# Written orders for the first two and last three head groups, a second set of probability tiles for the last group, and a shorter last row in a transposing attention kernel

## What is computed

```python
xn = layernorm(x)                                # x: 4 x 512 x 256, float32
Q = xn @ Wq + bq; K = xn @ Wk + bk; V = xn @ Wv + bv   # 16 heads of 128; 4 for K and V
attn = softmax(Q K^T / sqrt(128) + causal mask)
y = gelu((attn V) @ Wo + bo)
s = layernorm(xn + y) * gamma + beta
g = silu(ffn(xn))                                # gate/up 2 x 1024, down to 256
out = x + s * g
```

## Time and profile before

| | |
|---|---|
| median of the runs | 644.49 us (643.44, 648.06, 644.49) |
| profiled execution | 651.28 us, its span 649.5 us |
| mean granted TensorE clock | 0.978 |
| PE busy, PEld busy | 609.5 us (94%), 525.8 us (81%) |
| DVE, ACT, POOL busy | 479.2 us (74%), 428.7 us (66%), 304.1 us (47%) |

### The profile page before, as it was taken

How to read it: one execution, slowest core, us unless ns; L and a number is a source line. 1 busy time by engine, 2 the same in 40 slices (tenths; PEclk the granted TensorE clock), 3 DMA queues, 4 the chain that set the end, 5 groups by cost and what they waited for, 6 DMA issues and landing times.

```text
span 649.5 us, 10475 instructions
## 1 busy us (share of the span) xinstructions
PE 609.5 (94%) x3342; PEld 525.8 (81%) x3342; DVE 479.2 (74%) x1087; ACT 428.7 (66%) x1023; POOL 304.1 (47%) x243
## 2 busy tenths in 40 slices
PE   6899999999799999999999999999999999999771
PEld 4688888888678889788988888897988989798650
DVE  5654556543888778778988787898878889887736
ACT  2434344534788688677978777797877879787440
POOL 0000000000055654555689645468964546897544
...
GB/s 240 129 130 33 66 97 62 3 73 10 143 236 212 200 227 245 227 221 164 176 191 251 252 224 219 214 170 188 228 267 232 195 247 155 204 227 269 216 100 32
DMA packets 72501, 113.28 MB, mean 174 GB/s; under 512 B 11136, under 2 KB 50176, under 8 KB 70400
## 3 DMA queue, kind: packets, MB, share of 16 engines
...
q10 hardware_dynamic: 688, 0.33, 0.2%
...
## 4 chain that ended last, share of the span: by engine, by line
PE 62%; DMA 19%; DVE 7%; POOL 4%; ACT 4%; SPq 2%; issue 2%; ACTq 0%; POOLq 0%
PE bank L982 22%; PE down_ps L982 11%; DMA p_scratch<-probs 10%; PE down_ps L1112 8%; DMA probs<-p_scratch 7%; PE down_ps L1022 7%; PE bank L1011 6%; PE bank L1009 6%; POOL pT_lo L555 3%; DVE probs L915 3%; DMA raw<-in_wgu 2%; SPq L478 2%; PE bank L1073 2%; ACT pT_hi L698 1%; ACT probs L688 1%
## 5 line engine op out<-in xcount | busy, mean ns | idle before, releaser
L555 POOL TENSOR_TENSOR pT_lo<-probs,pT_hi 128x512 fp32r<-128x512 f32 x160 | 204.5, 1299 | 91.9 <-ACT pT_hi L698 91.4
L688 ACT ACTIVATE probs<-probs,least 128x512 f32<-128x512 f32 (+3 forms) x256 | 141.2, 554 | 37.6 <-DVE least L900 37.2
L900 DVE CUSTOM_DVE_ANT_0 probs<-bank,mask 128x512 f32<-128x512 f32 (+3 forms) x256 | 115.8, 484 | 24.9 <-PE bank L982 23.1
L698 ACT ACTIVATE pT_hi<-probs 128x512 fp32r<-128x512 f32 x160 | 96.1, 626 | 27.4 <-DMA probs<-p_scratch 21.1
L567 POOL TENSOR_TENSOR probs<-probs,inv 128x1024 f32<-128x1024 f32 (+1 forms) x32 | 47.0, 1469 | 141.1 <-DVE inv L908 141.0
L915 DVE STREAM_TRANSPOSE probs<-probs 128x2048 f32<-128x2048 f32 (+1 forms) x64 | 95.6, 1493 | 0.3 <-POOL probs L567 0.3
L1112 PE MATMUL down_ps<-wo_lo,cT_hi 128*128 128x256 f32 x256 | 74.4, 291 | 6.4 <-DVE cT_lo L940 6.3
L1112 PE MATMUL down_ps<-wo_hi,cT_lo 128*128 128x256 f32 x256 | 72.6, 284 | 0.0
L1112 PE MATMUL down_ps<-wo_hi,cT_hi 128*128 128x256 f32 x256 | 72.5, 283 | 0.0
L982 PE MATMUL down_ps<-pT_lo,v_hi 128*128 128x512 f32 x160 | 66.8, 417 | 6.0 <-POOL pT_lo L555 5.9
L982 PE MATMUL bank<-kT_lo,qT_hi 128*128 128x384 f32 (+1 forms) x192 | 66.4, 346 | 4.9 <-DVE least L900 3.3
...
## 6 DMA issues: line engine op xcount, KB each, us to landing
...
```

The costliest lines, as they stand in the source:

```text
L555: nc.gpsimd.tensor_tensor(lo[:].rearrange("p (a n) -> p a n", a=BLOCKS), turned(t, j), f32(hi[:]).rearrange("p (a n) -> p a n", a=BLOCKS), ...
L688: nc.scalar.activation(p, p, ACT.Exp, bias=least[:, u, g:g + 1], scale=-1.0, accum_out=total[:, n * T + t, g:g + 1]).then_inc(exp_done, 1)
L698: nc.scalar.activation(hi[:].rearrange("p (a n) -> p a n", a=BLOCKS), turned(t, j), ACT.Copy).then_inc(probsT_hi, 1)
L900: nc.vector.tensor_tensor_reduce(out=head_of(t, g), in0=ps[:, 0:(t + 1) * P].rearrange("p (k i) -> p k i", i=BLOCK), in1=mask_of(t), scale ...
```

## The change

The pattern stays for the middle. For the first two groups and the last three each engine gets a list of its own (`..._HEAD`, `..._TAIL`), and `program` puts them before and after what the pattern gives without them. What stands ahead of the last down product is now all of Q3, Q0, K, Q1, Q2; what stands ahead of `silu_out` on ScalarE is in `SCALAR_AHEAD`. The steps of the last row's end are in the lists too: `ty`, `ts`, `to` on VectorE (take y, statistics, output), `tg` (gelu), `tr` (root), `tp` (factors) and `td` (store).

The last group's probabilities get tiles of their own, in the space of Wq, with `gamma_g` and `beta_g`. Its masks so wait for the last projection and no longer for the `pl` of group 14. For the end, GpSimd makes g gamma and g beta + x ahead (`tile_factors`, three operations for each tile), and VectorE ends every tile with two operations.

```diff
+TENSOR_AHEAD = """
+Q3 Q0 K Q1 Q2
+"""
...
+SCALAR_AHEAD = """
+qh3 qh0 kh qh1 qh2 e2.0 e3.2 e3.1 e3.3 e3.0 e1.0 e2.2
+"""
...
+TRANSFER_HEAD = """
+W3 IW3 R3 W2 IR3 W0 IW2 R2 W1 IR2 R0 R1 W3+ R3+ W2+ IW3+ R2+ W1+ IR3+ W0+ IW2+ R1+
...
+def program(head, text, tail):
+
+    head, tail = [*listed(head, 0, 0)], [*listed(tail, LAST, B - 1)]
+    return head + [s for s in order(text) if s not in head and s not in tail] + tail
...
+    late = ExitStack()
+    probs_last = [sb(f"probs_last{t}", [P, G * (t + 1) * P], F32, late) for t in range(T)]
+    gamma_g = sb("gamma_g", [P, T, D], F32, late)
+    beta_g = sb("beta_g", [P, T, D], F32, late)
+    late.close()
     wq_s = pair("wq", [P, DC, H * E])
...
+        def tile_factors(t):
+
+            i = TILE_READY["tp", t]
+            pool.wait_ge(proj_done, max(PROJECTED["Q", LAST, h] for h in range(G)))
+            pool.wait_ge(g_b_in, 16 * B)
+            pool.wait_ge(x_b_in, 16 * B)
+            nc.gpsimd.tensor_tensor(beta_g[:, t, :], g_b[:, t, :], beta_row, ALU.mult).then_inc(tile_chain_pool, 1)
+            nc.gpsimd.tensor_tensor(gamma_g[:, t, :], g_b[:, t, :], gamma_row, ALU.mult)
+            pool.wait_ge(tile_chain_pool, i)
+            nc.gpsimd.tensor_tensor(beta_g[:, t, :], beta_g[:, t, :], x_b[:, t, :], ALU.add).then_inc(tile_ready, 1)
...
-        first = first_of("kh", "qh")
-        steps(ACT_STEPS[:len(first)])
+        steps(ACT_STEPS[:len(ACT_AHEAD)])
         silu_out(B - 1)
-        steps(ACT_STEPS[len(first):])
-        tile_gelu_of(1)
-        tile_gelu_of(0)
+        steps(ACT_STEPS[len(ACT_AHEAD):])
...
         def tile_output(t):
...
             r = res[:, t, :]
...
-            nc.vector.scalar_tensor_tensor(r, r, mv3[:, t, 0:1], gamma_row, ALU.subtract, ALU.mult).then_inc(tile_scaled, 1)
-            dve.wait_ge(tile_scaled, done + 1)
-            nc.vector.scalar_tensor_tensor(r, r, rstd3[:, t:t + 1], beta_row, ALU.mult, ALU.add).then_inc(tile_scaled, 1)
-            dve.wait_ge(tile_scaled, done + 2)
-            nc.vector.tensor_tensor(r, r, g_b[:, t, :], ALU.mult).then_inc(tile_scaled, 1)
-            dve.wait_ge(tile_scaled, done + 3)
-            nc.vector.tensor_tensor(r, r, x_b[:, t, :], ALU.add).then_inc(tile_out_dve, 1)
+            dve.wait_ge(tile_ready, TILE_READY["tp", t])
+            dve.wait_ge(tile_root, TILE_ROOT["tr", t])
+            nc.vector.scalar_tensor_tensor(r, r, mv3[:, t, 0:1], gamma_g[:, t, :], ALU.subtract, ALU.mult).then_inc(tile_scaled, 1)
+            dve.wait_ge(tile_scaled, TILE_OUT["to", t])
+            nc.vector.scalar_tensor_tensor(r, r, rstd3[:, t:t + 1], beta_g[:, t, :], ALU.mult, ALU.add).then_inc(tile_out, 1)
...
-                    if n and t in BY_DRAM:
+                    if n == LAST:
+                        dve.wait_ge(proj_done, max(PROJECTED["Q", n, h] for h in range(G)))
+                    elif n and t in BY_DRAM:
                         dve.wait_ge(probsT_split, PT_SPLIT["pl", n - 1, t, t])
```

More of the change, by code:

```diff
@@ new lines @@
+"""
+SCALAR_HEAD = """
+e0.2 e2.3 e0.3 vh3 e0.0 e1.2 e2.1 e1.3 e0.1 vh0 e1.1 vh1 kh+ qh3+ ph3.1 ph3.0 qh1+ ph3.2 qh2+ vh2 ph3.3 qh0+
+ph2.0 ph2.1 ph2.2 e3.2+ ch3 e3.3+ e3.1+ e3.0+ ph1.0 ph1.1 ph0.0 ch2 e2.3+ e1.0+ e1.2+ e1.3+ e2.0+ e2.2+ e2.1+
+e1.1+ e0.1+ kh++ e0.3+ e0.2+ e0.0+ ch1 qh0++ ph3.0+ ph3.2+ qh2++ ph3.1+ qh1++ ph3.3+ ch0
+"""
+SCALAR_TAIL = """
+qh3-- ph2.0--- ph2.1--- e3.1-- ph2.2--- e3.2-- ch3--- e3.3-- ph1.0--- e3.0-- ph0.0--- ph1.1--- gelu- e0.2--
+e1.1-- e2.3-- e2.1-- e2.2-- ch2--- e2.0-- e0.3-- e1.3-- e1.2-- e1.0-- e0.0-- qh2- ch1--- e0.1-- ph3.0-- qh0- kh-
@@ new lines @@
+"""
+POOL_HEAD = """
+no0 no1 pl3.1 pl3.0 pl3.2 pl3.3 pl2.0 pl2.1 pl2.2 pl1.0 pl1.1 pl0.0 no1+ no0+ pl3.0+ pl3.2+ pl3.1+ pl3.3+
+"""
+POOL_TAIL = """
+pl2.0--- pl2.1--- pl2.2--- pl1.0--- pl0.0--- pl1.1--- res- no1-- root- pl3.0-- no0-- pl3.1-- pl3.2-- pl3.3--
+pl2.0-- pl2.1-- pl2.2-- out0- pl1.0-- pl1.1-- pl0.0-- out1- out2- out3- out4- out5- no1- out6- pl3.0- out7-
+pl3.1- no0- pl3.2- pl3.3- pl2.0- pl2.2- pl2.1- pl1.0- no1 pl1.1- pl0.0- tp0 pl3.1 pl3.0 no0 pl3.2 pl3.3 pl2.0
+pl2.1 pl2.2 pl1.0 pl1.1 tp3 pl0.0 tr3 tp1 tr2 tp2 tr1 tr0
@@ L113, in order, with listed @@
                 yield (kind, n + shift, *which)
-def first_of(*kinds):
-    return [(kinds["KQ".index(step[0])], *step[1:]) for step in FIRST]
+def listed(text, kv, row):
+    for kind, which, shift, _ in words(text):
+        if kind in AT_END:
+            yield (kind, *which)
+        else:
+            yield (kind, (row if kind in TILE_ROWS else kv) + shift, *which)
 def ranks(steps, *kinds):
@@ L129, in ring_of @@
     return {s: (i % RING_BANKS, uses[i - RING_BANKS] if i >= RING_BANKS else None) for i, s in enumerate(uses)}
-def ahead(steps, first):
-    return [*first, *(s for s in steps if s not in first)]
-PE_STEPS = ahead(order(TENSOR_ORDER), list(FIRST))
-ACT_STEPS = ahead(order(SCALAR_ORDER), first_of("kh", "qh"))
-DVE_STEPS = ahead(order(VECTOR_ORDER), first_of("kl", "ql"))
-POOL_STEPS = list(order(POOL_ORDER))
-SP_STEPS = list(order(TRANSFER_ORDER))
+def program(head, text, tail):
+    head, tail = [*listed(head, 0, 0)], [*listed(tail, LAST, B - 1)]
+    return head + [s for s in order(text) if s not in head and s not in tail] + tail
+PE_AHEAD, ACT_AHEAD = [*listed(TENSOR_AHEAD, 0, 0)], [*listed(SCALAR_AHEAD, 0, 0)]
+PE_STEPS = program(TENSOR_AHEAD + TENSOR_HEAD, TENSOR_ORDER, TENSOR_TAIL)
+ACT_STEPS = program(SCALAR_AHEAD + SCALAR_HEAD, SCALAR_ORDER, SCALAR_TAIL)
+DVE_STEPS = program(VECTOR_HEAD, VECTOR_ORDER, VECTOR_TAIL)
+POOL_STEPS = program(POOL_HEAD, POOL_ORDER, POOL_TAIL)
+SP_STEPS = program(TRANSFER_HEAD, TRANSFER_ORDER, TRANSFER_TAIL)
+TILE_Y = ranks(DVE_STEPS, "ty")
+TILE_GELU = ranks(ACT_STEPS, "tg")
+TILE_VAR = ranks(DVE_STEPS, "ts")
+TILE_ROOT = ranks(POOL_STEPS, "tr")
+TILE_READY = ranks(POOL_STEPS, "tp")
+TILE_OUT = ranks(DVE_STEPS, "to")
 RING = ring_of(PE_STEPS)
@@ L264, in build, with probs_of, by_blocks, head_of @@
     ctx_banks = [down_ps[:, 2, :], down_ps[:, 3, :]]
[L266 to L270 removed]
+    def probs_of(n, t):
+        return (probs_last if n == LAST else probs)[t]
+    def by_blocks(n, t):
+        return probs_of(n, t)[:].rearrange("p (k g i) -> p k g i", g=G, i=BLOCK)
+    def head_of(n, t, g):
         if t in BY_DRAM:
[L273 to L278 removed]
+            return by_blocks(n, t)[:, :, g]
+        return probs_of(n, t)[:].rearrange("p (g k i) -> p g k i", g=G, i=BLOCK)[:, g]
+    def turned(n, t, j):
+        return probs_of(n, t)[:].rearrange("p (a j n) -> p j a n", a=BLOCKS, n=G * BLOCK)[:, j]
     def mask_of(t):
@@ L577, in _ @@
                 root(step[1])
+            elif step[0] == "tr":
+                tile_root_of(step[1])
+            elif step[0] == "tp":
+                tile_factors(step[1])
             else:
                 out_piece(step[2])(step[1])
-        def tile_root_of(t):
-            pool.wait_ge(tile_var, T - t)
-            nc.gpsimd.tensor_tensor(rstd3[:, t:t + 1], ve3[:, t:t + 1], neghalf[:, 0:1], ALU.pow).then_inc(tile_root, 1)
-        def tile_end(t):
-            n = POOL_TILES.index(t)
-            pool.wait_ge(tile_normed, n + 1)
-            pool.wait_ge(g_b_in, 16 * B)
-            r = res[:, t, :]
-            for i, (other, op) in enumerate(((gamma_row, ALU.mult), (beta_row, ALU.add), (g_b[:, t, :], ALU.mult))):
-                nc.gpsimd.tensor_tensor(r, r, other, op).then_inc(tile_chain_pool, 1)
-                pool.wait_ge(tile_chain_pool, 3 * n + i + 1)
-            nc.gpsimd.tensor_tensor(r, r, x_b[:, t, :], ALU.add).then_inc(tile_out_pool, 1)
-        tile_root_of(3)
-        tile_end(3)
-        tile_root_of(2)
-        tile_root_of(1)
-        tile_root_of(0)
-        tile_end(2)
     @block.scalar
```

144 lines of the change are left out of this document (77 added, 67 removed).

## The result

| | before | changed |
|---|---|---|
| runs (us) | 643.44, 648.06, 644.49, 645.95 | 656.32, 657.02, 658.38, 658.85 |
| median | 645.22 | **657.70** |
| ratio, 95% interval | | **1.0166** (1.0137 to 1.0195) |
| profiled execution, its span | 651.28, 649.5 | 656.32, 654.5 |

Slower by 1.7%, and 4.7 us above the top of the range. The changed kernel, run again beside other executions of before, gave 1.0146 (1.0107 to 1.0185).

The account below looks back on a forecast made before the run. TensorE's matmuls were taken to bound the middle, so only the ends could move: +8.5 (start) +0.5 (last three groups) -7.5 (end) = +1.5, 652.8 us profiled, 646.0 us median; range 638 to 651.

Parts of the forecast that it names:

- The start: First groups of attention: late silu and SP's wait for g's store delay the first probabilities; +8.5 us by group 1's end.
- The last three groups: Groups 13 to 15: late waits in group 13, then little movement; +0.5 us, between -6 and +5.
- group 14 gets them back: Last groups: the some 4 us TensorE loses in group 13 were to be regained in group 14.
- the row nearest is the write at 595.49, and it moves little: Last group's tile 3 write: forecast near 597.5 against 595.5, or 606 with the start's loss.
- xn stays where VectorE waits for its load: Last row's normalisation on VectorE: said to stay where VectorE waits for its load; no cost priced.
- The end: After the last matmul: earlier take of y and two operations per tile, 7.0 against 14.5 us; -7.5, between -6 and -9.
- The base: Whole kernel: summed against the profiled execution of 651.28 us, its 6.8 us above the median carried over as it was.
- ScalarE's in-order list: Slower rival, last groups: tile 3's `ch` behind tile 1's `ph` costs groups 14 and 15 too; +6.5, 651 us; chance 0.27.
- The store of g does not hold the start: Rival at the start: SP's wait is hidden, so the start gains 1 instead of losing 8.5; 636.5 us; chance 0.06.
- Much faster: Rival, last groups: transfers keep up, TensorE's waits and low clock go; start costs 6.5, tail gives 6; 637.5 us; chance 0.14.
- TensorE idle for 3 to 5 us before its first P: Sign at the start: this idle time was to show before the first product of probabilities, near 193.
- The middle: Sign between the ends: bound by TensorE, to stay as long as now; giving time back would show the forecast wrong.

Follow-up runs that it names:

- silu_early: Changed kernel with the last row's silu back right behind the projections on ScalarE, ahead of the seven exps; 650.48 us, ratio 1.0034.
- store_later: Changed kernel with SP storing g only ahead of the write of group 0's tile 2, the silu still late; 654.19 us, ratio 1.0072.
- tail_end: end_only plus the new lists for the last three groups and the last group's own probability tiles; 645.08 us, ratio 0.9967.
- end_only: Kernel before with its orders and shared probability tiles kept, only the last row's end taken from the change; 643.26 us, ratio 0.994.
- tail_xn: tail_end with VectorE normalising the last row behind group 14's last low part, not ahead of the scaling of its tile 3; 646.54 us, ratio 0.9966.
- tail_ch: tail_end with ScalarE's high part of group 13's tile 3 context moved ahead of the two high parts of tile 1; 645.21 us, ratio 0.9932.
- tail_both: tail_end with the moves of tail_ch and tail_xn together; 645.33 us, ratio 0.9938.
- repaired: Changed kernel with the edits of silu_early and tail_ch; 646.68 us, ratio 0.9997.

## Why the prediction was wrong

**The sum was +1.5, and the parts make about +8.** The ratios, 1.0166 and 1.0146, are 10.7 and 9.5 us; so some 2 us lie in no part. The second interval (6.9 to 12.0 us) holds the 8, the first (8.8 to 12.6) just misses it. By the table, against the kernels that keep before's lists for the stretch in question:

- *The start, +8.5: right in mechanism, 1.6 to 3 too small.* Every step is in the trace: g stored at 174.6 (175.0 forecast), the write at 178.25 (178.0), the first P at 193.92 (193), the pattern's first Q at 217.1 (217). silu_early and store_later show that it is the silu and SP's wait. What was mis-sized is the part behind it: I took 0.8 of 1.5 us for the second group and nothing after the pattern begins, but 1.3 us at S1.2 of group 2 (row above) and 0.7 to 1.3 before P3.0 of group 1 come after, in kernels with the early silu too. The stretch to P3.0 of group 3 takes 104.0 to 106.0 in the ten kernels with before's orders there, and 114.4 and 115.9 in the two profiles of the changed kernel.
- *The last three groups, +0.5: this is the step that failed.* It measured +4.2 by the two profiles and +5.4 by tail_end against end_only; up to the last matmul, where all kernels have done the same steps, +4.5 (+6.3 in the second profile) and +5.6. The value lay at my bound of +5. The step read: group 13 pays 4 us "and group 14 gets them back", since "the row nearest is the write at 595.49, and it moves little". The first wait came as forecast, 2.98 us with ScalarE's high part of the context behind tile 1's, and the write came at 606.34 against 606. That hit is partly luck: the change had cost 7.8 us up to P3.0 of group 12, not 8.5, so the write moved by 3.0 us in the tail and not by 2. And nothing was given back. I had priced each write of tile 3 and not VectorE's list in group 14, where 3.66 us of normalisation and 1.74 of transposition stand ahead of the low part that O3 waits for: 3.01 us. "xn stays where VectorE waits for its load" was wrong twice: the four operations moved ahead of that low part, and in neither kernel does VectorE idle before them. tail_xn shows that taking them away buys no time either, since the products of group 15 then wait for their transfers (2.21 and 2.99 us at ScalarE); the DMA share is 0.99 between 600 and 620 us. So the loss has two covers, one over the other, and I looked under neither. tail_ch takes away some 2 us of it, at group 13; for the rest, some 3 us up to the last matmul in tail_ch, tail_both and repaired against end_only, the cause stays open.
- *The end, -7.5: right in size (-7.7), by luck in part, and not independent.* end_only gives half of it, 3.7 us. The other half is work on tiles 3 and 2 done before the last matmul, while TensorE waits for it: its last O waits 2.42 us (1.6 before) for a low part that stands on VectorE behind an output and a statistic. A term measured from the last matmul counted as a gain what the term before it paid. From P3.0 of group 13 to the end it is 92.8 before, 88.2 with end_only and 89.5 changed (91.4 in the second profile).
- *A reading.* The wait of 3.88 us was taken for one for the last group's turned probabilities. Its row names the low part of group 14's context (`cT_lo`), for O1 of group 14; only the 2.07 is for turned probabilities. It stayed at 3.88 in every kernel with the orders of before, with tiles of the last group's own too.
- *The base.* I carried the profile's distance over the median (6.8) as it was. Three runs were too few: 645.22 and 644.49 stand against 647.2 to 649.4 from 17 to 24. That put the forecast some 3 us low in absolute terms (5 by the chip with 649.4); the ratio doesn't suffer.

**The rivals.** The slower one, "ScalarE's in-order list", had 0.27, a sum of +6.5 and 651. Its mechanism was the right one for group 13, and tail_ch supports it with 2.3 us and a wait of 1.43 in place of 2.68; for group 14 it names the wrong engine, since the wait of 3.01 is VectorE's. With the start at 10 its sum would have been +8, what the parts make. "The store of g does not hold the start" is refuted by store_later. "Much faster" needed the transfers to keep up; their share was already 0.95 in the earlier trace rows and is 0.99 now, and with the new lists none of TensorE's time was gained.

**The signs that were named.** "TensorE idle for 3 to 5 us before its first P" was 6.37; the last matmul came at 647.8, not 644; the 6.7 us after it were as forecast. The middle was 2.0 us shorter than before's, which was named as a sign of being wrong; but with identical lists it varies from 259.1 to 263.1, and before's profile is the longest.
